# Graph attention on one core: x loaded in row halves by two queues, the first weight slab in two pieces, and two of its preparation steps on other engines

## The reference, cut to what matters

```python
h = relu(layernorm(x))                       # x is 384 x 1024
q, k, v = (h @ w.T + b for w, b in ((wq, bq), (wk, bk), (wv, bv)))
q2, k2, v2 = (a @ w.T + b for a, w, b in ((q, wiq, biq), (k, wik, bik), (v, wiv, biv)))   # 16 heads of 64
scores = q2 @ k2.T / 8 + mask                # mask: built from 6528 typed edges, -inf where there is none
out = softmax(scores) @ v2                   # per head
y = x + out @ wo.T + bo
```

## Time and profile before

| | |
|---|---|
| device time, median of 3 runs (lowest to highest) | 295.41 us (295.35 to 295.54) |
| the profiled execution's own time | 295.47 us |
| its span in the profile | 293.7 us |
| TensorE busy | 287.4 us, 98% of the span |
| mean granted TensorE clock | 0.998 of full |
| VectorE, ScalarE, GpSimd busy | 176.7, 153.5, 150.7 us |

### The profile page before, as it was taken

The page is one execution under the profiler, slowest core; times in us unless marked ns, Lnnn a source line. Parts: engine busy times, 40 slices in busy tenths (PEclk is TensorE's granted clock), DMA queues, the critical chain, the costliest instruction groups (busy, mean ns, idle before and its releaser), DMA issues.

```text
span 293.7 us, 4994 instructions
## 1 busy us (share of the span) xinstructions
PE 287.4 (98%) x1813; PEld 266.4 (91%) x1813; DVE 176.7 (60%) x475; ACT 153.5 (52%) x288; POOL 150.7 (51%) x153
## 2 busy tenths in 40 slices
PE   6899999999999999999999999999999999999996
PEld 3699998888899999999999999999999997888885
DVE  4999778786544534454467766665747475835241
ACT  2876443152523443244324685969687879874100
POOL 6552455543464455545300797758393939874000
PEclk9999999999999999999999999999999999999999
DMA  7978955749733443334654043140403132400032
GB/s 257 332 230 264 315 191 180 232 153 301 270 105 117 139 143 136 91 134 145 182 193 145 0 141 106 46 144 0 145 10 136 41 106 71 144 1 2 0 143 71
DMA packets 15818, 40.84 MB, mean 139 GB/s; under 512 B 3481, under 2 KB 4914, under 8 KB 15794
## 3 DMA queue, kind: packets, MB, share of 16 engines
q1 hardware_dynamic: 13346, 38.53, 39.2%
q0 software_dynamic: 2016, 1.21, 1.8%
q10 hardware_dynamic: 432, 0.79, 0.7%
HBM read 37.71 MB, written 2.81 MB: 138 GB/s over the span
## 4 chain that ended last, share of the span: by engine, by line
PE 95%; DMA 2%; ACT 1%; DVE 0%; SPq 0%; issue 0%
PE banks L849 27%; PE banks L850 26%; PE banks L851 26%; PE banks L966 5%; PE banks L1009 3%; PE banks L1010 3%; PE banks L981 3%; DMA x_sb<-in_x 2%; PE banks L994 1%; PE banks L894 1%; PE banks L922 1%; PE banks L929 0%; PE banks L923 0%; ACT x_sb L476 0%; SPq L289 0%; DVE stats L679 0%
## 5 line engine op out<-in xcount | busy, mean ns | idle before, releaser
L403 POOL DMA_INDIRECT cells<-value,cell x51 | 54.8, 1074 | 59.2 <-DMA cells<-value,cell 45.9
L456 ACT ACTIVATE w_hi<-raw 128x1024 fp32r<-128x1024 f32 x51 | 53.8, 1055 | 17.5 <-PE banks L851 17.3
L849 PE MATMUL banks<-a_hi,w_hi 128*128 128x384 f32 x184 | 61.5, 334 | 0.0
L850 PE MATMUL banks<-a_hi,w_lo 128*128 128x384 f32 x184 | 61.5, 334 | 0.0
L851 PE MATMUL banks<-a_lo,w_hi 128*128 128x384 f32 x184 | 61.5, 334 | 0.0
L712 DVE TENSOR_TENSOR w_lo<-raw,w_hi 128x1024 fp32r<-128x1024 f32 x36 | 44.0, 1223 | 12.6 <-ACT w_hi L456 12.5
L429 POOL TENSOR_SCALAR prob<-prob,row_inv 128x384 f32<-128x384 f32 x36 | 22.5, 640 | 43.6 <-DVE row_inv L779 43.6
L374 POOL TENSOR_TENSOR w_lo<-raw,w_hi 128x1024 fp32r<-128x1024 f32 x15 | 36.0, 2404 | 0.9 <-ACT w_hi L456 0.9
L849 PEld LDWEIGHTS banks<-a_hi,w_hi 128*128 128x128 f32 x184 | 34.5, 188 | 0.1
L850 PEld LDWEIGHTS banks<-a_hi,w_lo 128*128 128x128 f32 x184 | 34.5, 188 | 0.0
L851 PEld LDWEIGHTS banks<-a_lo,w_hi 128*128 128x128 f32 x184 | 34.5, 188 | 0.0
(11 more groups left out here) (146 smaller groups left out, 610.1 us busy)
## 6 DMA issues: line engine op xcount, KB each, us to landing
raw<-in_slabs SPq DMA_DIRECT2D x56, 512.0 KB, 3.4
work<-key_rows SPq DMA_DIRECT2D x6, 256.0 KB, 5.3
prob<-key_rows SPq DMA_DIRECT2D x6, 256.0 KB, 3.8
x_sb<-in_x SPq DMA_DIRECT2D x3, 512.0 KB, 6.0
out_y<-x_sb SPq DMA_DIRECT2D x5, 256.0 KB, 2.1
cells<-prob SPq DMA_DIRECT2D x2, 576.0 KB, 7.9
cells<-value,cell POOLq DMA_INDIRECT x51, 2.6
x_sb<-in_x ACTq DMA_DIRECT2D x3, 256.0 KB, 4.3
```

The costliest lines, as they stand in the source:

```text
L403: nc.gpsimd.indirect_dma_start(out=cells[c][:, :], out_offset=bass.IndirectOffsetOnAxis(ap=cell[:, t:t + 1], axis=0), in_=value[:, t:t + 1 ...
L456: nc.scalar.activation(split_place(s)[0], raw[:, s % RAW, :], ACT.Copy).then_inc(slab_hi, 1)
L849: nc.tensor.matmul(psum, w[0], a[0], start=first, stop=False)
L850: nc.tensor.matmul(psum, w[1], a[0], start=False, stop=False)
```

## The change

x's half tiles are each loaded as two transfers of 64 rows, rows 0 to 63 by SyncE's queue and rows 64 to 127 by ScalarE's, in the order tile 0 left, tile 0 right, tile 1 left and so on; each half tile's semaphore now counts to 32. Slab 0 is loaded in two halves: the left one by SyncE between tile 1 and tile 2 of x (its own semaphore `half_in`), the right one behind x, without the wait for x's first half tile. ScalarE's `w_hi` of the left half moves ahead to behind its relu of tile 0. Its low part moves from GpSimd to VectorE, and the scaling of the last tile's right half moves from VectorE to ScalarE, behind `a_hi[1]`. ScalarE's split of slab 1 moves from behind `a_hi[4]` to behind `a_hi[3]`. TensorE transposes blocks 4 to 7 behind the three matmuls of k = 1, and its warm-ups are 15, 4 and 0 instead of 18, 4 and 3.

```diff
-WARM = [18, 4, 3]
+WARM = [15, 4, 0]
...
+        def load_x(eng, t, b, high):
+
+            own, half = slice(high * D, (high + 1) * D), slice(b * HALF, (b + 1) * HALF)
+            eng.dma_start(x_sb[own, t, half], x[t * P + high * D:t * P + (high + 1) * D, half]).then_inc(x_in[t][b], 16)
...
             for t in range(NT):
-                sp_eng.dma_start(x_sb[:, t, 0:HALF], x[t * P:(t + 1) * P, 0:HALF]).then_inc(x_in[t][0], 16)
+                if t == NT - 1:
+                    sp_eng.dma_start(raw[:, 0, 0:HALF], slabs[0, :, 0:HALF]).then_inc(half_in, 16)
+                for b in range(2):
+                    load_x(sp_eng, t, b, 0)
...
                 if s == 0:
-                    sp_eng.wait_ge(x_in[0][0], 16)
-                sp_eng.dma_start(raw[:, s % RAW, :], slabs[s]).then_inc(slab_in[s % RAW], 16)
+                    sp_eng.dma_start(raw[:, 0, HALF:F], slabs[0, :, HALF:F]).then_inc(slab_in[0], 16)
+                else:
+                    sp_eng.dma_start(raw[:, s % RAW, :], slabs[s]).then_inc(slab_in[s % RAW], 16)
...
-            for b in range(2):
-                half = slice(b * HALF, (b + 1) * HALF)
-                pool.wait_ge((half_hi, early_hi)[b], 1)
-                nc.gpsimd.tensor_tensor(w_lo[:, 0, half], raw[:, 0, half], w_hi[:, 0, half].bitcast(F32),
-                                        ALU.subtract).then_inc((half_lo, slab_lo)[b], 1)
+            pool.wait_ge(early_hi, 1)
+            nc.gpsimd.tensor_tensor(w_lo[:, 0, HALF:F], raw[:, 0, HALF:F], w_hi[:, 0, HALF:F].bitcast(F32),
+                                    ALU.subtract).then_inc(slab_lo, 1)
...
+                act.wait_ge(half_in, 16)
+                nc.scalar.activation(w_hi[:, 0, 0:HALF], raw[:, 0, 0:HALF], ACT.Copy).then_inc(half_hi, 1)
+
+            def scale_last(part, done):
+
+                nc.scalar.activation(x_sb[:, NT - 1, part], x_sb[:, NT - 1, part], ACT.Copy,
+                                     scale=rstd[:, NT - 1:NT]).then_inc(done, 1)
...
             for t in range(NT):
-                act.dma_start(x_sb[:, t, HALF:F], x[t * P:(t + 1) * P, HALF:F]).then_inc(x_in[t][1], 16)
...
+                for b in range(2):
+                    load_x(act, t, b, 1)
+            for t in range(NT - 1):
+                act.wait_ge(shift_ok, t + 1)
+                nc.scalar.activation(x_sb[:, t, :], x_sb[:, t, :], ACT.Relu, scale=rstd[:, t:t + 1],
+                                     bias=shift[:, t:t + 1]).then_inc(h_ok, 1)
+                if t == 0:
+                    first_slab_hi()
...
+            act.wait_ge(h_step, 1)
+            act.wait_ge(rstd_ok, NT)
+            scale_last(slice(0, HALF // 2), h_ok)
+            scale_last(slice(HALF // 2, HALF), h_ok)
             for k in range(KT):
                 act.wait_ge(h_turned, k + 1)
                 nc.scalar.activation(a_hi[:, k, :], h_bank[k][:, 0:N], ACT.Copy).then_inc(h_hi, 1)
-                if k == KT // 2:
+                if k == 1:
+                    act.wait_ge(h_step, 2)
+                    scale_last(slice(HALF, F), h_last_ok)
+                if k == KT // 2 - 1:
                     split_hi(1)
...
-                    dve.wait_ge(x_in[t][b], 16)
+                    dve.wait_ge(x_in[t][b], 32)
...
-            dve.wait_ge(rstd_ok, NT)
-            dve.wait_ge(h_step, 2)
-            nc.vector.tensor_scalar(h_last, h_last, rstd[:, NT - 1:NT], None, ALU.mult).then_inc(h_last_ok, 1)
+            dve.wait_ge(half_hi, 1)
+            nc.vector.tensor_tensor(w_lo[:, 0, 0:HALF], raw[:, 0, 0:HALF], w_hi[:, 0, 0:HALF].bitcast(F32),
+                                    ALU.subtract).then_inc(half_lo, 1)
...
-                    if k == 0:
+                    pe.wait_ge(h_lo, k + 1)
+                    mm = nc.tensor.matmul(psum[:, 0:N], hi[:, c], a_lo[:, k, :], start=False, stop=(k == KT - 1))
+                    if k == 1:
                         pe.wait_ge(h_last_ok, 1)
                         for late in range(KT // 2, KT - 1):
                             turn_h(late, NT - 1)
```

More of the change, by code:

```diff
@@ L177, in gat_kernel @@
         x_in = [[sem(f"x_in{t}_{b}") for b in range(2)] for t in range(NT)]
+        half_in = sem("half_in")
         slab_in = [sem(f"slab_in{r}") for r in range(RAW)]
@@ L463, in first_slab_hi @@
             def first_slab_hi():
-                half = slice(0, HALF)
-                act.wait_ge(slab_in[0], 16)
-                nc.scalar.activation(w_hi[:, 0, half], raw[:, 0, half], ACT.Copy).then_inc(half_hi, 1)
-            for t in range(NT):
-                act.dma_start(x_sb[:, t, HALF:F], x[t * P:(t + 1) * P, HALF:F]).then_inc(x_in[t][1], 16)
-            for t in range(NT):
-                if t == NT - 1:
-                    first_slab_hi()
[L474 to L483, removed]
+                act.wait_ge(half_in, 16)
[3 more added lines that the diff above has]
+                                     scale=rstd[:, NT - 1:NT]).then_inc(done, 1)
+            for t in range(NT):
+                for b in range(2):
[5 more added lines that the diff above has]
+                if t == 0:
+                    first_slab_hi()
+            act.wait_ge(h_step, 1)
+            act.wait_ge(rstd_ok, NT)
+            scale_last(slice(0, HALF // 2), h_ok)
+            scale_last(slice(HALF // 2, HALF), h_ok)
             for k in range(KT):
@@ L927, in first_tile @@
                             turn_h(late, NT - 1)
-                    pe.wait_ge(h_lo, k + 1)
-                    mm = nc.tensor.matmul(psum[:, 0:N], hi[:, c], a_lo[:, k, :], start=False, stop=(k == KT - 1))
-                    if k == 0:
                         for t in range(NT):
```

## The result

The changed kernel takes 298.94 us (median of 6 runs, 298.05 to 300.59) against 295.39 us (6 runs, 295.27 to 295.55). The ratio is 1.0121, 95% interval 1.0104 to 1.0137: 3.5 us slower, where 295.4 and a range up to 296.3 were forecast. The profiled execution took 298.96 us, with a span of 297.2.

What follows compares the result with a forecast made beforehand. TensorE was taken as the bound, through slab 1's first matmul at 17.07. 0.23 us earlier at `a_hi[0]`, given back as two waits for VectorE's low parts, net 0.0 against 295.47, gave 295.4 us, range 294.8 to 296.3.

Steps and rivals of the forecast that it cites:

- What bounds the kernel now: TensorE, busy 287.4 of 293.7 us; the change is worth what it moves slab 1's first matmul, at 17.07.
- Tile 0's statistics: VectorE's first statistics: left half lands near 3.3, second statistics at 4.05 to 4.1, tiles 0 and 1 up to 0.53 earlier.
- Tile 2's transfer is the term that decides: Last tile of x: halves taken to land at 7.6 and 7.9, so its second statistics start at 8.27, 0.16 earlier.
- The issues: ScalarE's queue: six issues instead of three ahead of its first work, taken as hidden.
- ScalarE up to the scaling: Moved `w_hi` waits for slab 0's piece; relu of tile 1 still ends 0.7 before the scaling, so hidden.
- What is put behind `a_hi[0]`, and TensorE's first tile: Added scaling and earlier split on ScalarE; TensorE waits for low parts at k = 0 and 4, first tile 11.87 to 17.08.
- The clock: Rival: fewer warm-ups let TensorE's clock fall to 1.2 GHz before the first tile, 1.6 us more, 297.0; chance 0.10.
- The rival of late data: Slab 0's piece makes tile 2 late: statistics at 8.05 and 8.72, 0.45 later, 295.9; chance 0.17.

Runs made afterwards that it cites:

- e3: The kernel before with only x's half tiles as two 64-row transfers by the two queues: 297.51 us, ratio 1.0085.
- e13: The kernel before with only slab 0's left half as its own transfer between tile 1 and tile 2 of x: 296.67 us, ratio 1.0038.
- e15: The kernel before with x in six 256 KB transfers of 64 adjacent rows, rows 0 to 63 by SyncE, 64 to 127 by ScalarE: 297.73 us, ratio 1.0102.
- e1: The changed kernel with x's half tiles again as single 128-row transfers, left by SyncE, right by ScalarE: 298.11 us, ratio 1.009.
- e10: The kernel before with only the moved work and TensorE's new order; transfers in the order of before, warm-ups 18, 4, 3: 296.18 us, ratio 1.0025.
- e5: The changed kernel with the transfers in the order of before; moved work and 15, 4, 0 warm-ups stay: 295.86 us, ratio 1.0013.
- e6: The changed kernel with transfers in the order of before, but no wait for x's first half tile ahead of slab 0: 296.00 us, ratio 1.0019.
- e4: The changed kernel with the warm-ups of before, 18, 4 and 3: 298.15 us, ratio 1.0088.
- e14: The kernel before with 64-row transfers for tile 0 of x alone, tiles 1 and 2 as before: 297.24 us, ratio 1.0058.
- e16: The kernel before with x in six 256 KB transfers of 64 rows, even and odd rows on the two queues: 296.48 us, ratio 1.0034.
- e9: The kernel before with only the warm-ups changed, 15, 4, 0 instead of 18, 4, 3: 295.54 us, ratio 1.0040.

## Why the prediction was wrong

- **What bounds the kernel now:** right. The whole loss is what slab 1's first matmul moved, 3.53 of 3.55 us, and TensorE gets no wait of note behind it.
- **Tile 0's statistics:** wrong. The left half of a tile was to land near 3.3; the second statistics were to start at 4.05 to 4.1. They started at 4.05 and 5.06. The step took 400 GB/s, a rate of 128-row transfers, for transfers of 64 rows. The rule of the Trainium skill against two transfers to partition halves was named and given no price but the 0.53 us gain; it was the rule to follow, and its price was a slower stream for all of x.
- **Tile 2's transfer is the term that decides:** it did, and this is the step that failed: the time at which tile 2 lands. Its bounds, 6.95 to 8.05 for the left and 7.25 to 8.55 for the right half, both came from bytes at before's rate plus before's lag. The statistics started at 9.37 and 10.51. Missing were the rate with 64 rows (e3: 1.6 us later than before, by itself) and the slow stretch behind the piece (e13: 1.3 us, where its bytes account for 0.66). Why that stretch is slow stays open.
- **The issues:** "six issues instead of three" were counted at nothing. They take 0.6 to 0.7 us each, not 0.38 to 0.46, so SyncE's last of x was issued at 4.4. That is not the bound in e15, whose issues end at 2.9.
- **ScalarE up to the scaling:** right, the moved `w_hi` is hidden. Overlooked was VectorE's order: tile 1's shift stands behind tile 2's left statistics, so a late tile 2 makes tile 1's relu late too and leaves TensorE idle ahead of the first tile (e1).
- **What is put behind `a_hi[0]`, and TensorE's first tile:** right in place, small in size. The waits came at k = 0 and k = 4; 0.24 us were worked out for the first tile (5.21 against 4.97), e10 measured 0.45. It also has no earlier `a_hi[0]` to pay with (11.59 against 11.46): e10 is 0.7 us slower.
- **The clock:** the mechanism was right, the trigger half right. The forecast hung it on the warm-ups alone and gave it 0.10; with the data in time and 15, 4, 0 warm-ups it is 2 of 29 executions (e5, e6, e9). It also fell with the warm-ups of before (e4, e14, e15), but often only where late data and fewer warm-ups came together (12 of 17). It belongs to the cases in which x is late, not beside them. The 1.6 us priced for it are 1.3 in its stretch beside e5, and 1.02 at the end of the first tile. The forecast took the slow warm-ups of before, up to 5.92 us, for 1.2 GHz by their spacing alone: the granted clock in the earlier trace rows reads 1.00 there. That low pace lasts to 5.9 us before and to about 11.4 in e6, so its length in one trace was no fixed price.
- **The rival of late data** had the sign and the place, but its 295.9 had the same rate in it. The two rivals came together: in the profiled execution the first matmul is 2.02 us late, and the first tile takes 1.51 us more, 0.49 for the moved work and 1.02 for the half clock. That is the 3.53.

The parts alone (2.1 for the rows, 1.2 for the piece, 0.4 for moved work and warm-ups) add up to 3.7, near the 3.5. That is luck in part, since both transfer parts delay the same tile (undoing one leaves it at 10.1 to 10.5) and the clock makes up the rest. No version here beats the kernel before.

## What to carry to other kernels

Load with all 128 partitions in a transfer: halves of adjacent rows on two queues cost a third of the rate here, and many small transfers cost on their own. Before putting a transfer ahead of one on the path, price it above its bytes; 262 thousand bytes cost 1.3 us, not 0.66. Where the first data sets the start of a kernel that lives on TensorE, count late data twice, once as itself and once as the clock it may take along, above all when warm-ups go at the same time. Look also at what stands in an engine's program behind a wait for late data, as tile 1's shift does here; no run moved it, so what it is worth is not shown.

## What the runs showed of the hardware

- The DMA share doesn't tell this loss: 0.97 with 235 GB/s in e15, 0.99 with 362 in before. Read the GB/s beside it.
- A transfer of 64 rows took longer to issue than one of 128: 0.47 to 0.87 us in the changed kernel against 0.38 to 0.46 before, for half the bytes; with the same bytes (e15, e16) it is 0.57 to 0.88.
- The granted clock of a window can read 1.00 while matmuls keep the half pace: the first warm-ups of every trace here start 0.32 us apart, and in e6 that pace lasts until about 11.4 us.
- Taking away 6 of 25 warm-ups left most executions alone and made 4 of 10 longer by 2 to 4 us (e9), though e5 has the same warm-ups and nine of its ten runs lie within 295.74 to 296.05 (one at 301.80). How often it happens is thus known only roughly.
